# Expert stage of a four-layer block: step loops of two instead of four, two gathers in flight instead of four, and the second expert's low part made by VectorE

## The reference

```python
logits = x @ router_w + router_b
route = jax.nn.softmax(logits, axis=1)
max_prob = jnp.max(route, axis=1, keepdims=True)
max_ind = jnp.argmax(route, axis=1)
for e in range(num_experts):                 # 8 experts
    h = x @ w1[e]                            # 4096 x 256 by 256 x 2048
    a, g = jnp.split(h, 2, axis=1)
    y = jax.nn.silu(a) * g @ w2[e]           # 1024 -> 256
    out = jnp.where((max_ind == e)[:, None], y, out)
out = out * max_prob
```

## Time and profile before

| what | value |
|---|---|
| median of 3 runs | 1462.95 us (1462.44 to 1464.23) |
| span of the profiled execution | 1465.5 us (the page gives no other time of it) |
| PE busy | 1373.6 us, 94% of the span |
| DVE, ACT, POOL busy | 889.3, 658.5, 749.0 us |
| expert stage | from about 183.8 to 569 us |
| mean granted PE clock | 0.971 |

### The profile page before, as it was taken

The page is one execution under the profiler, slowest core; times in us unless marked ns, Lnnn a source line. Parts: engine busy times, 40 slices in busy tenths (PEclk is TensorE's granted clock), DMA queues, the critical chain, the costliest instruction groups (busy, mean ns, idle before and its releaser), DMA issues. The chain is left out here.

```text
span 1465.5 us, 29372 instructions
## 1 busy us (share of the span) xinstructions
PE 1373.6 (94%) x9361; PEld 1212.6 (83%) x9362; DVE 889.3 (61%) x1869; ACT 658.5 (45%) x1206; POOL 749.0 (51%) x693
## 2 busy tenths in 40 slices
PE   7997798999999995899988999999999998999998
PEld 3454687888888884677778999999999988999997
DVE  5787522332332333677578888888888864566656
ACT  4553432333333331666544444444444435555553
POOL 6663187765550002331039887987987957240400
PEclk9997799999999998899999999999999999999999
DMA  4111425232220002310033274474474587465450
GB/s 169 48 43 56 151 65 176 100 117 100 85 97 14 14 15 92 113 58 1 1 116 88 80 208 119 146 208 119 146 208 116 148 252 265 159 216 187 151 206 30
DMA packets 112543, 171.49 MB, mean 117 GB/s; under 512 B 6400, under 2 KB 97664, under 8 KB 106336
## 3 DMA queue, kind: packets, MB, share of 16 engines
q1 hardware_dynamic: 103456, 156.27, 33.1%
q0 software_dynamic: 3408, 9.31, 2.2%
q10 hardware_dynamic: 5616, 5.11, 1.0%
HBM read 115.22 MB, written 55.44 MB: 116 GB/s over the span
## 5 line engine op out<-in xcount | busy, mean ns | idle before, releaser
L2109 PE MATMUL comb_psO<-hand_parts,comb_eh 128*128 (+1 forms) x1024 | 198.7, 292 | 0.5 <-DVE comb_el L2228 0.3
L1774 ACT ACTIVATE disp_raw<-disp_psL 128x512 f32<-128x512 f32 x128 | 76.6, 598 | 198.7 <-PE disp_psL L1686 112.1
L2109 PEld LDWEIGHTS comb_psO<-hand_parts,comb_eh 128*128 128x128 f32 x1024 | 157.5, 190 | 1.1 <-DVE comb_el L2228 0.7
L1087 DVE TENSOR_TENSOR moe_hs<-moe_psH,moe_act_a 128x512 f32<-128x512 f32 x78 | 50.3, 686 | 178.0 <-PE moe_psH L981 144.1
L1686 PE MATMUL disp_psL<-disp_ph,hand_xh 128*128 (+1 forms) x512 | 147.8, 289 | 0.8 <-DVE disp_e L1959 0.8
L1686 PE MATMUL disp_psL<-disp_ph,hand_xl 128*128 (+1 forms) x512 | 145.0, 283 | 0.0
L1686 PE MATMUL disp_psL<-disp_pl,hand_xh 128*128 (+1 forms) x512 | 144.9, 283 | 0.0
L2109 PE MATMUL comb_psO<-hand_parts,comb_el 128*128 (+1 forms) x512 | 144.6, 282 | 0.0
L2228 DVE TENSOR_TENSOR comb_el<-comb_psT,comb_eh 128x512 fp32r<-128x512 f32 x128 | 88.0, 689 | 91.3 <-ACT comb_eh L2143 88.8
L1710 PE MATMUL disp_psS<-disp_e,last_x 128*128 128x256 f32 x512 | 132.8, 382 | 3.8 <-POOL disp_e L1868 3.8
L1185 POOL DMA_INDIRECT lin_yg<-sorted_y,table_place x32 | 32.5, 1015 | 191.4 <-POOLq L896 143.3
(11 more groups left out here) (287 smaller groups left out, 3919.6 us busy)
## 6 DMA issues: line engine op xcount, KB each, us to landing
logits<-disp_raw SPq DMA_DIRECT2D x64, 512.0 KB, 4.0
hand_e<-logits SPq DMA_DIRECT2D x32, 1024.0 KB, 6.3
w_raw<-in_w SPq DMA_DIRECT2D x8, 2048.0 KB
disp_wt<-in_w_slot SPq DMA_DIRECT2D x16, 1024.0 KB, 9.9
w_raw<-in_w SPq DMA_DIRECT2D x8, 1024.0 KB
slot_y<-disp_slots SPq DMA_DIRECT2D x64, 128.0 KB, 3.2
disp_bt<-in_b_slot SPq DMA_DIRECT2D x15, 512.0 KB, 4.9
comb_y_in<-slot_y SPq DMA_DIRECT2D x3, 2048.0 KB, 10.5
```

What stands on the lines that cost most here:

```text
L1087: v.tensor_tensor(hs[:, cols], psH[:, 2 + h, :], act_a[:, cols], ALU.mult).then_inc(hs_ready, 1)
L1774: nc.scalar.activation(raw[mc % 4][:, half * 2:half * 2 + 2, :], psL[l_bank[mc]][:, half * 2:half * 2 + 2, :], ACT.Copy).then_inc(copied, 1)
L2109: last = nc.tensor.matmul(psO[j % 2][:, 0:D], ep[s % EB][:, i, :], yp[:, bass.ds(odd, 1), ch * D:(ch + 1) * D].rearrange("p a d -> p (a d) ...
```

## The change

`FLIGHT` gathers, 2 instead of 4, may be under way; the semaphores become 2. The pipeline's loop body holds two steps, so that the loop covers steps 4 to 37 in 17 passes and branches back 16 times, and 38 to 40 are written out. The 32 low pieces of expert 1 leave POOL and go to DVE, at the end of steps 0 to 3 (8, 4, 8 and 12 pieces). SP's first wait asks for the same eight landings as before.

```diff
 FIRST_GATHERS = 1
+FLIGHT = 2
...
-        self.landed = [m.sem(f"gathered{i}") for i in range(4)]
+        self.landed = [m.sem(f"gathered{i}") for i in range(FLIGHT)]
...
-        q = slot % 4
-        wait(pool, self.landed[q], 16 * (slot // 4))
+        q = slot % FLIGHT
+        wait(pool, self.landed[q], 16 * (slot // FLIGHT))
...
-    def low_chunk(self, pool, e, n):
+    def low_chunk(self, dve, e, n):
...
-        pool.wait_ge(self.high, 2 * (e - 1) + part + 1)
-        last = self.nc.gpsimd.tensor_tensor(lo[:, e, cols], raw[:].rearrange("p k f -> p (k f)")[:, cols], hi[:, e, cols].bitcast(F32),
+        dve.wait_ge(self.high, 2 * (e - 1) + part + 1)
+        last = self.nc.vector.tensor_tensor(lo[:, e, cols], raw[:].rearrange("p k f -> p (k f)")[:, cols], hi[:, e, cols].bitcast(F32),
                                             ALU.subtract)
...
             for t in range(4):
-                step(t, t % 4)
-            with eng.Fori(1, SLOTS // 4) as i:
-                for q in range(4):
-                    step(i * 4 + q, q)
-            for t in range(SLOTS // 4 * 4, SLOTS + 2):
-                step(t, t % 4)
+                step(t, t % 2)
+            with eng.Fori(2, SLOTS // 2) as i:
+                for q in range(2):
+                    step(i * 2 + q, q)
+            for t in range(SLOTS // 2 * 2, SLOTS + 2):
+                step(t, t % 2)
...
-        AHEAD = 4
+        LOWS = (8, 4, 8, 12)
...
-            for q in range(4):
-                sp.wait_ge(gathered[q], 32)
+            for q in range(FLIGHT):
+                sp.wait_ge(gathered[q], 64)
...
                 gathers.issue(pool, slot)
-                if slot >= AHEAD:
-                    for n in range(2 * (slot - AHEAD), min(2 * (slot - AHEAD) + 2, w.LOW_CHUNKS)):
-                        w.low_chunk(pool, 1, n)
...
+                if isinstance(s, int) and s < len(LOWS):
+                    for n in range(sum(LOWS[:s]), sum(LOWS[:s + 1])):
+                        w.low_chunk(dve, 1, n)
```

More of the change, by code:

```diff
@@ L1034, in fetch @@
             def fetch(t, q):
-                act.wait_ge(gathered[q], before(t, q, 4) + 16)
+                act.wait_ge(gathered[q], before(t, q, 2) + 16)
                 wait(act, x_turned, t)
@@ L1066, in step @@
                 if live(t):
-                    fetch(t, (q + 1) % 4)
+                    fetch(t, 1 - q)
             tiles(act, step)
```

## The result

The changed kernel takes 1466.13 us (median of 22 runs, 1462.53 to 1469.07) where the kernel before, run with it, takes 1463.76 us (22 runs, 1459.86 to 1467.05). The ratio is 1.002, with an interval of 1.0013 to 1.0027: 1.9 to 4.0 us slower. The forecast was 1461.6 us, 1.3 us under the 1462.95 us that the kernel before had then. The time lies inside the range of 1456.5 to 1467, but it moved the other way.

What follows compares the result with a forecast made beforehand. The prediction took PE to bound the expert stage. Earlier split of expert 2 (-2.4), back branches behind tile 8 (+2.4) and less half clock (-1.3) summed to -1.3 us: 1462.95 to 1461.6 us, range 1456.5 to 1467.

Steps and rivals of the forecast that it cites:

- Is the stall there in the timed runs?: Expert stage: likelier reading that timed runs lack the profiled 9.96 us stall and have a 4.5 us PE wait instead.
- the hidden wait: PE at tile 8, the first of expert 2: without the stall it would wait 4.5 us for `w_lo`.
- The stall itself: PE between the silus of tiles 5 and 6: 9.96 us lost, but worth at most 5.4 us if removed.
- What POOL and the load gain: POOL's gathers and expert 2's split: one gather per 1.5 us, split ready at 263.1 instead of 265.5, -2.4 us.
- rival 3: POOL's gathers become the bound: 3.4 us landing, pace 1.75, +7.9 us, 1470.9 us; decides from about 1.6; chance 0.13.
- The clock term: PE around tile 8: a shorter wait is less likely to bring a half-clock stretch; -1.3 us, bounds 0 and 4.
- The back branches: PE's queue: 16 loop branches instead of 7 at 0.30 us each, +2.7 us, of which +2.4 behind tile 8.
- The low pieces on DVE: DVE in steps 0 to 3: the pieces fit its idle time before each `moe_hs`, cost 0.
- Rival 4: DVE's pieces slow POOL's gathers through shared SBUF interfaces; would change little; no separate chance given.
- Rivals 1 and 2: Stall is in timed runs: it goes, 1457.5 us, chance 0.22; or stays or moves, 1463.3 or 1473.3 us, chance 0.10.

Runs made afterwards that it cites:

- second trace of the kernel before: The kernel before profiled again with nothing changed: 1462.31 us (8 runs) against 1463.76 us for the same kernel beside it, ratio 0.9987.
- the body of four: The changed kernel with the loop body of four steps again, two gathers in flight, low pieces on DVE: 1463.7 us, ratio 1.0006 to the kernel before.
- the first trace: The kernel before, unchanged, in the profiled execution the prediction was read from: span 1465.5 us, timed median 1462.95 us.

## Why the prediction was wrong

**"Is the stall there in the timed runs?" Right.** The second trace of the kernel before has no stall and has the hidden wait behind it, 3.97 us against 4.5 predicted. The argument for it was weaker than its result: runs of one kernel spread by 3 us to either side, so a median 2.55 us under a span says little. In the profiled runs with a time beside the span the time is 1.7 to 2.2 us above the span (1465.28 and 1463.4 for the body of four, for instance). The stall itself was worth 3.3 us and not 5.4: from the silu of tile 0 to that of tile 8 the first trace takes 85.14 us and the second 81.88, since the wait behind the stall brings a stretch at the lower clock with it.

**"What POOL and the load gain": the step that failed, by its size.** The forecast was a gather every 1.5 us and POOL free at 250.5, 2.4 us earlier. The changed kernel issues 21 more gathers between 184.91 and 219.87, one per 1.66 us, three in the 11.7 us up to 231.53 under the load, and 13 more up to 252.78, one per 1.63. (The load started at 218.53, forecast 218. It held the gathers up for less time than the 15 us taken, which hid part of the error.) Counted from the silu of tile 0, POOL is free 253.19 - 189.49 = 63.7 us later in the second trace of before and 253.73 - 189.43 = 64.3 us later in the changed kernel. The term of -2.4 came out as +0.6.

The landing was not what was mis-sized. The forecast took 2.9 us; the 34 gathers that do not meet the load take 3.0 us on the mean (2.7 to 3.9, median 2.8). What the forecast had wrong is the step from the landing to the pace. With two in flight two gathers go per round, and a round was taken as little more than a landing, 3.0 us. It measures 3.3 (2 x 1.65): a waiting gather starts 0.2 to 0.3 us after the landing that it waits for, and some start later still, because the gather ahead of them was late. The one at 187.91 follows a landing at 184.91 + 2.7 = 187.6. The one at 193.28 follows one at 192.2, but stands 1.25 us behind its late neighbour at 192.03. This is rival 3's mechanism at its turning point, a pace of about 1.6 us, where it had "the rest is the +2.4 of the branches". It came without the landing of 3.4 us that rival 3 asked for. The case had got 0.13; it should have been the middle of the forecast.

**The clock term, -1.3: about -0.7, and not for the reason given.** It stood on a shorter wait. But PE waits 4.24 us in the changed kernel, and its clock falls there too. What the low clock costs is the distance from the silu of tile 7 to that of tile 8 less a step of 9.44 and less the wait: 15.94 - 9.44 - 3.97 = 2.5 us in the second trace of before, 15.53 - 9.44 - 4.24 = 1.9 in the changed kernel. It does not follow the wait: with the body of four it is 1.8 after 4.74 us, and with two gathers in flight alone 1.8 after 12.10 us. The second trace of before is the one that stands apart: its matmuls stay slow for 4.9 us behind the wait (265.97 to 270.83), those of the changed kernel for 3.4. So the 0.7 us are luck of single executions, as far as these traces show.

**The back branches, +2.7 (2.4 behind tile 8): right.** From tile 8 to tile 38 the second trace of before takes 556.33 - 271.37 = 284.96 us, the changed kernel 558.26 - 271.23 = 287.03: +2.07 for eight, 0.26 each. The ninth is before tile 8, hidden in the wait. From tile 0 to tile 8 it is 81.88 and 81.80 us, the +0.6 and the -0.7 of the two terms above. The sum is +0.6 - 0.7 + 2.07 = +2.0 us where the forecast had -1.3, and lies inside the 1.9 to 4.0 of the timed runs; the loop of four brings the time back to 1463.7. What the Trainium skill (Runtime: NRT & Kernel Launch, Instruction fetch mechanics) says against loops holds in its direction: every branch back costs PE, and written out the stage is fastest. That a fetch is what a branch pays for is not shown: with nine more branches the changed kernel's page counts 61 packets on the two instruction queues, where the kernel before has 63.

**The low pieces on DVE, 0: right.** They take 2.78, 1.42, 2.22 and 2.50 us, forecast 2.8, 1.4, 2.3 and 2.6, and PE waits for none. Rival 4's mechanism shows, and is small: three of POOL's gathers take 1.13 to 1.21 us where 0.95 is usual (187.91, 196.29, 207.59), and all three start while DVE makes pieces. That is 0.6 us on POOL in all, some of it under waits.

**Rivals 1 and 2** fell with the stall. What the prediction did not ask is what each part would do alone. By the stage, moving the pieces off POOL gains 6.4 us with four gathers in flight and 7.5 with two (374.36 against 366.83). Two in flight cost 7.5 us with the pieces on POOL (10.0 by the medians, 1473.21 against 1463.22) and 6.4 without them (366.83 against 360.42). The change does both to the same queue, and they cancel: 366.83 against 366.84 with the body of four. The loop of two steps costs the rest, 2.0 us.

## What to carry to other kernels

When a stall that only one trace shows is taken out of the sum, work out which wait it was hiding, and get a second trace before pricing either. Where a queue is made lighter and its DMAs are throttled in the same change, price the throttle by the distance from issue to issue, and not by the landing alone: here the landing was 3.0 us, nearly as forecast, but a round of two gathers took 3.3. With a limit of two, 0.15 us for each of 34 gathers is 5 us, more than the whole expected gain. And try each part of a compound change alone: here one part gains 6.4 us and another takes it back. A loop's back branch on an engine that never idles has a price of its own (0.3 us here), and halving the body doubles their number.

## What the runs showed that was not expected

One profiled execution of the kernel before lost 9.96 us between two silus, with idle gaps of 0.89 us between PE's matmuls, while no other trace here, the same kernel's included, shows such a stall. Its cause stays open. A back branch to a body of eight steps costs PE some 0.4 us where one to a body of two or four costs about 0.3; the traces do not say why. In all four traces with a wait of PE at tile 8, of 3.97 to 12.10 us, a stretch at the 1.2 GHz level follows and costs 1.8 to 2.5 us, no more after the longest wait than after the others. In the second trace of before the clock is low from the first matmul after the wait, in the changed kernel from 0.8 us after its end.
